# Cross-attention and routed FFN on one core: seven units' attention exponentials through tanh, and one exponential for their router

## What is computed

```python
# cross attention; x is 4 x 1024 x 256, the context 4 x 77 x 256
h = tanh(txt_proj[:, None, :, :] + feat_proj[:, :, None, :] + b)   # 4 x 1024 x 77 x 256
rho = einsum('bftd,d->bft', h, w) + (1.0 - qm)[:, None, :] * NEG
att = softmax(rho, axis=-1)
txt_h = einsum('bft,btd->bfd', att, textual_features)
w_s = tanh(txt_h @ Wcw + bcw); b_s = tanh(txt_h @ Wcb + bcb)
x = x + w_s * features + b_s                 # features = layernorm(x)
# routed FFN on layernorm(x): 8 experts, each takes its 512 best of 4096 tokens
probs = softmax(x @ gate, axis=-1)
scores, token_idx = top_k(probs transposed, k=512)
routed = scatter_add(gelu(tok @ W1 + b1) @ W2 + b2, scaled by scores)
out = x + routed + gelu(x @ Ws1 + bs1) @ Ws2 + bs2
```

## Time and profile before

| what | value |
|---|---|
| median of 3 runs | 893.86 us (893.48 to 893.88) |
| span of the profiled execution | 892.1 us |
| ACT busy | 767.8 us, 86% |
| PE busy | 801.3 us, 90% |
| DVE busy | 708.7 us, 79% |
| ACT_TABLE_LOADs | 12 |

### The profile page before, as it was taken

One profiled execution on the slowest core, in us unless ns is written; L12 is line 12 of the kernel. 1 busy time (PEld: TensorE's weight loads), 2 busy tenths in 40 slices (PEclk: granted clock), 3 DMA queues, 4 the chain that ended last, 5 costly groups with the idle time before them and its releaser, 6 DMA issues.

```text
span 892.1 us, 14125 instructions
## 1 busy us (share of the span) xinstructions
PE 801.3 (90%) x5385; PEld 472.7 (53%) x5385; DVE 708.7 (79%) x1405; ACT 767.8 (86%) x601; POOL 307.6 (34%) x537
## 2 busy tenths in 40 slices
PE   7975679569998999999999999999988999999996
PEld 5321123124443444445454455545766899999986
DVE  5899889898989689988878995894887877676641
ACT  3989999999999999999999999997753677676672
POOL 3310540615543007674002740052203145555424
PEclk9899999999999999999999999999999999999998
DMA  8000000000001000200000010002202365544513
GB/s 267 19 1 0 1 1 1 1 24 15 10 9 40 1 1 25 71 2 1 24 1 1 25 48 1 24 1 89 77 24 78 98 181 142 136 106 132 137 20 41
DMA packets 32406, 41.82 MB, mean 47 GB/s; under 512 B 2365, under 2 KB 29011, under 8 KB 32339
## 3 DMA queue, kind: packets, MB, share of 16 engines
q1 hardware_dynamic: 26083, 32.49, 10.9%
q0 software_dynamic: 6144, 8.39, 5.7%
q10 hardware_dynamic: 112, 0.04, 0.0%
HBM read 28.33 MB, written 12.58 MB: 46 GB/s over the span
## 4 chain that ended last, share of the span: by engine, by line
PE 39%; ACT 38%; issue 11%; DVE 9%; POOL 1%; DMA 0%; POOLq 0%; ACTq 0%; DVEq 0%
ACT z L995 31%; PE bank L914 10%; PE bank L937 9%; PE bank L787 7%; DVE z L1372 4%; PE bank L829 3%; PE bank L844 3%; ACT z L991 2%; ACT u L1038 2%; PE bank L763 2%; PE bank L715 1%; PE bank L952 1%; PE bank L817 1%; ACT L1038 1%; PE bank L888 1%
## 5 line engine op out<-in xcount | busy, mean ns | idle before, releaser
L995 ACT ACTIVATE z<-z 128x4096 f32<-128x4096 f32 (+5 forms) x157 | 520.9, 3364 | 4.6 <-DVE z L1372 4.4
L1372 DVE TENSOR_SCALAR z<-feat,txt_bias 128x1024 f32<-128x1024 f32 (+1 forms) x722 | 421.9, 656 | 36.5 <-PE bank L787 35.6
L787 PE MATMUL bank<-z,window 128*32 128x512 f32 x2464 | 304.9, 604 | 64.0 <-ACT z L995 62.5
L787 PEld LDWEIGHTS bank<-z,window 128*32 128x32 f32 x2464 | 70.0, 110 | 249.7 <-issue 134.1
L844 PE MATMUL bank<-ws_sb,u 128*128 128x256 f32 x512 | 126.3, 387 | 5.6 <-ACT u L1038 5.6
L844 PEld LDWEIGHTS bank<-ws_sb,u 128*128 128x128 f32 x512 | 92.2, 189 | 41.1 <-issue 19.8
L829 PE MATMUL bank<-tr,ws_s 128*128 128x512 f32 x384 | 107.9, 417 | 0.0
L914 PE MATMUL bank<-xg_s,w_s 128*128 128x512 f32 x384 | 99.5, 397 | 0.2 <-DVE xg_s L1672 0.2
L937 PEld LDWEIGHTS bank<-w_s,hid_s 128*128 128x128 f32 x672 | 86.3, 188 | 4.0
L937 PE MATMUL bank<-w_s,hid_s 128*128 128x256 f32 x672 | 88.2, 280 | 0.0
L1074 ACT ACTIVATE hid<-bank,vec 128x512 f32<-128x512 f32 x64 | 44.2, 690 | 49.3 <-PE bank L914 49.2
(11 more groups left out here) (264 smaller groups left out, 750.4 us busy)
## 6 DMA issues: line engine op xcount, KB each, us to landing
w_raw<-in_L_ffn_W_dram SPq DMA_DIRECT2D x16, 1024.0 KB, 5.6
x_ring<-in_x_dram SPq DMA_DIRECT2D x8, 512.0 KB, 7.9
xn_dram<-xn SPq DMA_DIRECT2D x8, 512.0 KB, 2.9
out_dram<-x_ring SPq DMA_DIRECT2D x8, 512.0 KB, 3.2
u<-in_L_ffn_Ws_dram SPq DMA_DIRECT2D x1, 1024.0 KB, 11.0
ws_sb<-in_L_ffn_Ws_dram SPq DMA_DIRECT2D x1, 1024.0 KB, 13.7
xg<-xn_dram,idx POOLq DMA_INDIRECT x32, 4.1
out_dram<-y,idx POOLq DMA_INDIRECT x32, 3.9
```

Source lines behind the costliest of these rows:

```text
L787: ins = e.matmul(sums[v][32 * r:32 * r + 32, :], window[:, c, 31 - k:63 - k], z[:, n % ZB, at_piece:at_piece + TOK], start=(v, r) not in b ...
L995: e.activation(part, part, ACT.Tanh).then_inc(signal(*step), 1)
L1372: ins = e.tensor_scalar(z[:, n % ZB, i * width:(i + 1) * width], feat_of(units, c), bias_of(units, t, c), None, ALU.add)
```

## The change

Three things are changed. First, `att_exp` of units 0 to 6 becomes a tanh with scale -0.5, and `weigh` of these units closes the exponential on DVE: with t = tanh(-x/2), exp(x) = 2/(1 + t) - 1, so three DVE instructions on 128 x 320 numbers come ahead of the four that were there (add 1, reciprocal, multiply by 2 and subtract 1). Second, the router's exponentials of units 0 to 6 are one instruction on 128 x 224 (`early_exp`) behind the last tanh block, with `early_sums` and `early_probs` on DVE in place of seven `router` steps. Third, POOL's `values` is one pass over all 32 tiles behind the last router step; before it was 24 tiles during the tanh blocks and 8 tiles at the end. The first function table is now the one that has gelu and tanh. Unit 7 keeps its Exp.

```diff
--- before.py
+++ after.py
@@ -131,9 +131,6 @@
                 [("gate_in", v)], [("gates", v)], [("y_scale", v)], [("logits_shift", v)],
                 [("y_norm", v), ("store_xn2", v)], [("y_turn", v, c) for c in range(C)],
                 *[[("y_turned", v, c)] for c in range(C)], [("whole", v, j) for j in range(J)]]
-
-    def probs_of(v):
-        return [[("logits_exp", v)], [("router", v)]]
 
     def down_ends(v):
         steps = [("down_end", v, half) for half in range(2)]
@@ -166,13 +163,8 @@
         base, early, late = starts[bb], early - UPB, late - UPB
         at_slots(ends_at[early] + 1, TAIL_EARLY if early else TAIL_FIRST, tail(early))
         at_slots(base, TAIL_LATE, tail(late))
-        for v in ([early - UPB, late - UPB] if bb > 1 else []):
-            at_slots(base, (3, 5), probs_of(v))
     base = ends_at[va] + 1
     at_slots(base, TAIL_SINGLE, tail(va))
-    for v in (va - 2, va - 1):
-        at_slots(base, (2, 5), probs_of(v))
-    at_slots(base, (5,), [[("values", 0, NT - 2 * J)]])
     n = 0
     for v, (begin, step) in enumerate(FFN):
         for m in range(M):
@@ -248,14 +240,14 @@
 
     held += [step for step in lead if step[0] == "gelu"]
     late = {step[1:3] for step in held}
-    order += [("logits_exp", va), ("router", va), *end[0], *(step for step in lead if step[0] == "up"), *end[1],
-              ("load_w1", 0), ("load_w2", 0), *end[2], ("att_exp", vb)]
+    order += [("early_exp",), ("early_sums",), *end[0], *(step for step in lead if step[0] == "up"), *end[1],
+              ("load_w1", 0), ("load_w2", 0), *end[2], ("att_exp", vb), ("early_probs",)]
     order += [step for step in lead if step[0] == "down" and step[1:3] not in late]
     fill_chain(8)
     ends = [step for step in lead if step[0] in BY_VECTOR]
     order += [*ends[:1], *held[:GELUS_BEFORE], *end[4], *end[5], *ends[1:], *end[6], *held[GELUS_BEFORE:]]
     held.clear()
-    order += [*end[7], *end[9], *end[8], ("logits_exp", vb), ("y_shift_last", vb), ("router", vb), ("values", NT - 2 * J, NT)]
+    order += [*end[7], *end[9], *end[8], ("logits_exp", vb), ("y_shift_last", vb), ("router", vb), ("values",)]
     order += [step for step in lead if step[0] == "down" and step[1:3] in late]
     fill_chain(TAIL_FILL[0])
     order.append(("probs_turn",))
@@ -468,6 +460,9 @@
         bits = tested[:].bitcast(I32).rearrange("p (t e) -> p t e", e=E)
         rest = scan[:, 1, :].rearrange("p (t e) -> p t e", e=E)
         b2_raw = eq[0:B2_ROWS, :]
+        early_units = UNITS - 1
+        early_lg = lg[:, 0:early_units].rearrange("p v j e -> p (v j) e")
+        early_total, early_inverse = [eq[:, i * NT:i * NT + early_units * J] for i in range(2)]
         b2_s = sb("b2_s", [B2_ROWS, D], F32R)
         b2_row = sb("b2_row", [B2_ROWS, E + 1], F32R)
         idx = sb("idx", [P, NL, A], I32)
@@ -962,7 +957,7 @@
                 kind, args = step[0], step[1:]
                 if kind == "warm":
                     e.wait_ge(consts, 4)
-                    e.activation(spare[:, 1:2], spare[:, 0:1], ACT.Tanh).then_inc(signal(*step), 1)
+                    e.activation(spare[:, 1:2], spare[:, 0:1], ACT.Gelu_apprx_tanh).then_inc(signal(*step), 1)
                 elif kind == "vec_out":
                     e.wait_ge(*done("vec_turn"))
                     e.activation(vec[:], banks[UP[0]][:, 0:NV], ACT.Copy).then_inc(signal(*step), 1)
@@ -996,11 +991,17 @@
                 elif kind == "att_exp":
                     v, = args
                     e.wait_ge(*done("att_shift", v))
-                    e.activation(att[:, v % 2], att[:, v % 2], ACT.Exp).then_inc(signal(*step), 1)
+                    if v == vb:
+                        e.activation(att[:, v % 2], att[:, v % 2], ACT.Exp).then_inc(signal(*step), 1)
+                    else:
+                        e.activation(att[:, v % 2], att[:, v % 2], ACT.Tanh, scale=-0.5).then_inc(signal(*step), 1)
                 elif kind == "gates":
                     v, = args
                     e.wait_ge(*done("gate_in", v))
                     e.activation(wb[:, v % 2], wb[:, v % 2], ACT.Tanh).then_inc(signal(*step), 1)
+                elif kind == "early_exp":
+                    e.wait_ge(*done("logits_shift", va))
+                    e.activation(lg[:, 0:vb], lg[:, 0:vb], ACT.Exp).then_inc(signal(*step), 1)
                 elif kind == "logits_exp":
                     v, = args
                     e.wait_ge(*done("logits_shift", v))
@@ -1231,27 +1232,25 @@
                     e.affine_select(out=earlier_tile[:], in_=same_expert[:], compare_op=ALU.is_gt, fill=0.0, base=0,
                                     pattern=[[1, P]], channel_multiplier=-1).then_inc(signal(*step), 1)
                 elif kind == "values":
-                    first, end = args
-                    tiles = slice(first, end)
-                    shape = [P, end - first, E]
-                    if first == 0:
-                        e.wait_ge(consts, CONSTS)
-                    e.tensor_copy(vals[:, tiles, :, 0], tok_tile[:, tiles].unsqueeze(2).broadcast_to(shape))
-                    e.tensor_copy(vals[:, tiles, :, 1], tok_part[:, 0:1].unsqueeze(2).broadcast_to(shape))
-                    e.wait_ge(*done("router", end // J - 1))
-                    link(e.tensor_copy(vals[:, tiles, :, 2], probs[:, tiles, :]))
+                    shape = [P, NT, E]
+                    e.wait_ge(consts, CONSTS)
+                    e.tensor_copy(vals[:, :, :, 0], tok_tile[:].unsqueeze(2).broadcast_to(shape))
+                    e.tensor_copy(vals[:, :, :, 1], tok_part[:, 0:1].unsqueeze(2).broadcast_to(shape))
+                    e.wait_ge(*done("early_probs"))
+                    e.wait_ge(*done("router", vb))
+                    link(e.tensor_copy(vals[:, :, :, 2], probs[:]))
                     e.wait_ge(pool_link, linked)
-                    link(e.tensor_tensor(rest[:, tiles, :], probs[:, tiles, :], vals[:, tiles, :, 2], ALU.subtract))
+                    link(e.tensor_tensor(rest, probs[:], vals[:, :, :, 2], ALU.subtract))
                     e.wait_ge(pool_link, linked)
-                    link(e.tensor_copy(vals[:, tiles, :, 3], rest[:, tiles, :]))
+                    link(e.tensor_copy(vals[:, :, :, 3], rest))
                     e.wait_ge(pool_link, linked)
-                    e.tensor_tensor(vals[:, tiles, :, 4], rest[:, tiles, :], vals[:, tiles, :, 3],
+                    e.tensor_tensor(vals[:, :, :, 4], rest, vals[:, :, :, 3],
                                     ALU.subtract).then_inc(signal(*step), 1)
                 elif kind == "gather":
                     ex, = args
                     e.wait_ge(*done("folded", ex))
                     if ex == 0:
-                        e.wait_ge(*done("values", NT - 2 * J, NT))
+                        e.wait_ge(*done("values"))
                         e.wait_ge(stored[2], 16)
                         e.wait_ge(stored[3], 16)
                         for v in range(UNITS):
@@ -1436,6 +1435,13 @@
                     v, = args
                     a = att[:, v % 2]
                     e.wait_ge(*done("att_exp", v))
+                    if v < vb:
+                        link(e.tensor_scalar(a, a, 1.0, None, ALU.add))
+                        e.wait_ge(vector_link, linked)
+                        link(e.reciprocal(a, a))
+                        e.wait_ge(vector_link, linked)
+                        link(e.tensor_scalar(a, a, 2.0, -1.0, ALU.mult, ALU.add))
+                        e.wait_ge(vector_link, linked)
                     link(e.tensor_reduce(sm[:, v % 2, 1, :], a, AX.X, ALU.add))
                     e.wait_ge(vector_link, linked)
                     link(e.reciprocal(sm[:, v % 2, 2, :], sm[:, v % 2, 1, :]))
@@ -1511,6 +1517,19 @@
                     link(e.tensor_reduce(biggest, l, AX.X, ALU.max))
                     e.wait_ge(vector_link, linked)
                     e.tensor_tensor(l, l, biggest.unsqueeze(2).broadcast_to([P, J, E]), ALU.subtract).then_inc(signal(*step), 1)
+                elif kind == "early_sums":
+                    e.wait_ge(*done("early_exp"))
+                    e.wait_ge(*done("split_b2"))
+                    link(e.tensor_reduce(early_total, early_lg, AX.X, ALU.add))
+                    e.wait_ge(vector_link, linked)
+                    e.reciprocal(early_inverse, early_total).then_inc(signal(*step), 1)
+                elif kind == "early_probs":
+                    e.wait_ge(*done("early_sums"))
+                    known = slice(0, vb * J)
+                    link(e.tensor_tensor(probs[:, known, :], early_lg, early_inverse.unsqueeze(2).broadcast_to([P, vb * J, E]), ALU.mult))
+                    e.wait_ge(vector_link, linked)
+                    e.tensor_scalar(bits[:, known, :], probs[:, known, :].bitcast(I32), 31 - 2 * HALF_BITS, None,
+                                    ALU.logical_shift_left).then_inc(signal(*step), 1)
                 elif kind == "router":
```

(3 more changed lines are left out.)

## The result

The median is 900.58 us (900.28 to 902.3, four runs) against 893.85 (893.48 to 893.88, four runs): the ratio is 1.0079, with a 95% interval of 1.0065 to 1.0094. The kernel became slower by 0.8%, 6.7 us, where +2.5 us was forecast; the time lies just above the range. The profiled execution has a span of 898.7 us, 6.6 more than before.

What follows compares the result with a forecast made beforehand. ScalarE was taken as the bound, TensorE about 4% behind and VectorE some 10%. Steps 2.96 - 0.53 + 1.01 + 0.7 - 1.98 = +2.2, with +0.3 at the end +2.5 us: 893.86 + 2.5 = 896.3 us, range 889.0 to 900.0.

Steps and rivals of the forecast that it cites:

- The price E: VectorE time of the three closing instructions ahead of the gates, seven times: 2.96 us each, 2.5 to 3.4 beside it.
- one pass: Rival: the reciprocal is one pass like a sum, E 1.28 us, total -4.7 us, 889.2 us; chance 0.22.
- eight passes: Rival: the reciprocal takes eight passes a number, 2.82 us, E 3.62, total +7.1 us, 901.0 us; chance 0.11.
- TensorE takes up VectorE's delays: Rival: TensorE's backlog covers the late blocks at units 2 to 5, total +0.7 us, 894.6 us; chance 0.12.
- (1): Unit 0, block 37: ScalarE already waits for VectorE, no margin, the whole of E is lost: +2.96 us.
- (2): Unit 1: one load less gives 1.40 us, VectorE's margin is 2.09 us; net -0.53 us.
- (3): Units 2 and 3: ScalarE waits at the gates (0.55 us), unit 3's add comes later (0.46); together +1.01 us.
- (5): Unit 6: of the 3.04 us from two loads and the router pair 1.06 is lost; net -1.98 us.
- the 0.24: Router exponentials of a pair, made one instruction, cost 0.24 us beyond their overlap, at each of three tails.
- The cap of 2.3 us: Unit 6: TensorE can come forward by 2.3 us at most, from its waits for gelu (1.9) and a tanh (0.4).
- (4): Units 4 and 5 repeat units 2 and 3 with a margin of 2.70 us: 0.26 and 0.45, +0.7 us.
- The end: Behind the tanh blocks: later router and values work mostly hidden, counting tests slower beside POOL; +0.3 us (0 to 0.8).

Runs made afterwards that it cites:

- Experiment 4: Changed kernel with units 0 and 1 on Exp without closing and the earlier first table: 897.33 us, ratio 1.0028 to the kernel before.
- experiment 7: Changed kernel with all attention exponentials Exp, nothing closed, earlier first table; router exponentials merged, values in one pass: 892.66 us, ratio 0.998 to the kernel before.
- experiment 8: Changed kernel with tanh and closing for unit 6 alone, units 0 to 5 Exp, earlier first table: 890.91 us, ratio 0.9964 to the kernel before.
- experiments 1: Changed kernel without the three closing instructions for units 0 to 6 (computation left out): 886.22 us, ratio 0.9902 to the kernel before.
- 2: Changed kernel with the two cheap closing instructions kept and the reciprocal left out (computation left out): 886.76 us, ratio 0.9914 to the kernel before.
- Experiment 3: Changed kernel with unit 6's statistics two blocks earlier in VectorE's queue: 898.52 us, ratio 1.0037 to the kernel before.
- 5: Changed kernel with the gates of units 2 and 4 one block later in ScalarE's queue: 900.92 us, ratio 1.0056 to the kernel before.
- 6: Changed kernel with units 0 and 1 on Exp and unit 6's statistics two blocks earlier: 895.7 us, ratio 1.0021 to the kernel before.

## Why the prediction was wrong, step by step

**The price E was right.** 2.16 us for the reciprocal against 2.15 measured, 0.70 for the two cheap instructions against 0.65, in all 2.90 at unit 2 (334.06 to 336.96) against 2.96. Both rival prices fell with it: one pass (0.48) and eight passes (2.82). That TensorE takes up VectorE's delays fell too: the lag of the tanh passes on in full.

**Steps (1), (2), (3) and (5) were right** to within 0.45 us each. So was the reading behind them, which takes the instant when VectorE's output is ready and the instant when ScalarE comes for it. Experiment 4 shows (1) and (2) by taking them away, 7 the 0.24, and 8 shows (5) alone, -2.0 against -1.98 forecast. The 3.04 us for a tail with two loads is 3.08 in experiment 8, and the one load taken away at the first gelu gives 1.43 in experiments 1 and 2 (block 50), so 1.40 for a load was right. The 2.66 us for a switch of the Trainium skill, "ScalarE: Activation LUTs", section "What ACT_TABLE_LOAD costs", do not come out here.

In step (1) the lag is 2.89 at block 37, which is the price, and 0.34 more comes at blocks 39 and 43. TensorE waits 4.44 us for block 37 (1.54 before), and the granted clock is 0.50 from 159.5 to 166.3, where before it was whole. Experiments 3 and 5 have both again; no run parts them.

**Two smaller faults.** The cap of 2.3 us on unit 6's gain, from TensorE's waits, was wrong: this tail gives 3.1 in experiments 1, 2 and 8. It entered the one-pass rival and the lower end of my own range, not the sum. And the upper end of that range, +5.7, comes to +5.6 by its own terms.

**The failed step is (4)**, the sentence "Units 4 and 5 repeat it with a margin of 484.67 - 481.97 = 2.70". It gave +0.7 and measured +4.4. The margins in it were right: in experiments 3 and 6, where TensorE doesn't wait for GpSimd, the same blocks lose 0.85. I had asked at each closing what ScalarE would wait for, and not what else stands behind the closing in VectorE's queue. Between the tails of units 3 and 4 stands unit 6's `x_stat`, for which GpSimd waits, and for GpSimd's chain behind it TensorE waits. The chain measured, at block 100: 1.89 us of wait, and 5.33 - 3.64 = 1.69 us for `rho`, with 3.4 us of it at a granted clock of 0.50, together 3.6. The rows for this were in the trace of before: GpSimd waited for `x_mv` there (6.06), and `xn` was done at 394.85, 3.2 us ahead of the transposes at 398.04. Statistics 7.3 us later against transposes 4.1 later use up that slack. The wait of 1.89 is then the 2.0 us by which GpSimd's chain grew (1.2 of it the last step, 4.44 to 5.60). That it would grow could at most be guessed from its 0.20 and 0.58 us instructions in the trace of before; that the clock would fall behind the wait was in no row around that place. Experiment 3 removes the cause and both effects at the price of 1.3 us elsewhere, which makes this cause shown, and not argued.

A further stretch at a granted clock of 0.50, from 497.4 to 500.8, behind a wait of TensorE of 2.48 us, cost nothing that shows: the ends of `rho` are 0.7 us later behind it and come back, and the lag of the tanh stays 7.74 from block 124 to 127. The step to 8.53 at block 128 is a wait of 0.67 us for an add behind unit 5's closing, as at block 89 behind unit 3's. What stays open is why the clock fell behind the wait of 1.89 us at block 100, and the longer chain of GpSimd is read from rows, not tried.

**The end** was +0.3 by forecast and came out at -0.4; experiment 7, with -0.5, has the same end without any closing, and in the other experiments it lies between -0.3 and +0.15. Its parts were not timed apart, so whether a counting test got longer and something else gave more is open.

## What to carry to other kernels

When work goes from one engine to another, list everything behind it in the receiving engine's queue and find for each item who waits for it and with what slack, not only for the two engines that trade. Do it through one chain more than seems needed: here the cost came through VectorE, GpSimd and TensorE. An exchange that is about even in sum can still be worth making at the one place where its price is lowest: of the seven units, unit 6 had two loads to save for one closing and a margin for it, and the tanh at that unit alone, with the router's half, made the kernel 3.0 us faster, where the router's half alone gave 1.3.

## What the runs showed of the hardware

VectorE's reciprocal has a price per number of 6.2 ns (178, 328 and 2154 ns for 4, 28 and 320 numbers), six times that of a sum.

TensorE's granted clock went to 0.50 for 3.4 us after a wait of 1.89 us at block 100, and 32 matmuls that began in front of that stretch took 5.33 us where they take 3.64. The same came after 1.90 and 1.94 us there in experiments 4 and 5; after 1.30 and 0.52 us in experiments 1 and 2 it did not. The length of the wait alone doesn't tell: a wait of 1.81 us is followed by such a stretch at 517.56 in experiment 4 and by none at 520.4 in the changed kernel, and one of 1.94 at 184.0 before the change by none.

A small GpSimd instruction on 128 x 4 numbers took 0.58 to 0.60 us beside VectorE's adds and 0.20 with VectorE idle.

On ScalarE a table load of 1283 ns cost 1.4 us in the stream and the exponential behind it started at once, with nothing more for emptying the pipeline.
